# Sums of squares of four heads at once, in float32, on four 32-column groups of TensorE

## The chip, the cores and the metric

The kernel runs on one core of a Trainium2 chip. The metric is the time of one execution on the device, in microseconds (us). Tensors lie in SBUF as partitions by elements; TensorE writes into PSUM. The engines are TensorE (PE, its weight loads PEld), VectorE (DVE), ScalarE (ACT), GpSimd (POOL) and SyncE (SP), which here only issues DMAs.

## The reference, cut to what matters

```python
# x: 16 x 100 x 512, context: 16 x 361 x 256, 16 heads of 128
q = (layernorm(x) @ Wq).reshape(B, Sq, H, D)
k = (ctx @ Wk).reshape(B, Skv, H, D)
v = (ctx @ Wv).reshape(B, Skv, H, D)
q = q * rsqrt(mean(q**2, -1) + eps) * gq       # over the 128 of a head
k = k * rsqrt(mean(k**2, -1) + eps) * gk
attn = softmax(einsum(q, k) / sqrt(D))
x = x + (attn @ v).reshape(B, Sq, H * D) @ Wo
x = x + ffn(layernorm(x))                      # Hadamard, 8-bit activations, ternary weights
```

## The kernel before, in words

There are three stages, one after the other. The first, `queries`, goes over 4 groups of 4 batches (400 tokens) and in each over 16 heads. It makes the queries, stores them to DRAM, and makes the sum of squares of each query. The second, `attention`, goes over 64 units of four heads (16 batches of four units). The third, `feed_forward`, does the output projection and the feed-forward step. The first two are what the change touches.

Nearly all products take float32r operands, each split into a high and a low part: three matmuls (high by high, low by high, high by low) in place of one. psV (`values`), the transposes and a few others have plain float32 operands.

The head's 128 numbers lie on partitions, so the sum of squares is a matmul with a column of ones. Before the change it goes head by head, over four engines:

- ScalarE squares the product out of PSUM into `sq` (L402 in the queries, `square_k` L879 in the attention).
- VectorE casts it to float32r, `sq_hi` (L482, L1015).
- GpSimd subtracts to get the low part, `sq_lo` (L258, L707).
- TensorE runs two float32r matmuls of 128 columns of weights (`squares`, L299 and L766). The weights are a slice of `sel`, which is zero but for one column of ones, at a place that puts the sums of head h on row h of psS (psN in the attention); rows of other heads get zeros added. The heads so add up in one bank, and the last closes it.
- VectorE takes the rows as `ms` (L459, L1025). In the queries TensorE transposes them (psR, L308) to `rq_all`; in the attention SP sends them out and in again so that 76 partitions hold them (`ms_sp`), GpSimd raises them to the power -0.5 (L718), and SP brings the result to all queries as `rk`.

Each engine has its program written out, and the order is set by hand. In the attention a step (one head n) on TensorE is: scores of n (psS), keys of head n + 11 (psK, six matmuls), squares of head n + 9 (psN), transposes of n - 2 (psP), and then either a part of the values of unit u - 2 (psV, steps 0 and 1) or a half of the gather of unit u - 1 (psZ, steps 2 and 3). On ScalarE it is: pr of n - 1, the high part of the keys, the exponential of n, the square, the high part of the transposes. On VectorE: 1/sum of n - 1, ms (step 3), the low part of the transposes, the scaling of the scores with the maximum, the low part of the keys, the negated maximum, the cast. psK has two banks, `sq` two slots.

In the queries a step on TensorE is twelve matmuls for psQ and the squares of the head two before.

Of the kernel before, what the change touches and what calls it, by code (L numbers as in the profile page):

```python
# [22 lines left out]
P = 128  # L23
# [23 lines left out]
TT = P  # L47
TILES = -(-T // TT)
# [3 lines left out]
def build(nc, x, ctxT, ctx_k, wq, wk, wv, wo, gq, gk, w_ff, ident_in, had_in, out):  # L52
# [4 lines left out]
    with ExitStack() as top:  # L57
# [20 lines left out]
        with ExitStack() as ctx:  # L78
# [4 lines left out]
                "sel": sbt(ctx, "sel", [P, 2 * P - 1], F32R),  # L83
# [37 lines left out]
def queries(nc, sbt, sem, passed, weights, ident, rq_all, neg_half, asums, d_q, x, wq, wk, wv, gq, gk, w_ff, ctxT,  # L121
# [7 lines left out]
    with ExitStack() as ctx:  # L129
# [14 lines left out]
        sq = sb("sq1", [P, 2, GT])  # L144
        sq_hi, sq_lo = sb("sq1_hi", [P, 2, GT], F32R), sb("sq1_lo", [P, 2, GT], F32R)
        ms = sb("ms1", [H, GT])
# [3 lines left out]
        psR = ctx.enter_context(nc.psum_tensor("psR", [P, GB, H], F32))  # L150
# [10 lines left out]
        p_q, a_q, v_sqhi, g_sqlo = s("p1_q"), s("a1_q"), s("v1_sqhi"), s("g1_sqlo")  # L161
# [80 lines left out]
        def _(pool):  # L242
            nc.gpsimd.memset(neg_half[:], -0.5).then_inc(g_const, 1)
            nc.gpsimd.memset(sel[:].bitcast(F32), 0.0).then_inc(g_const, 1)
            pool.wait_ge(g_const, 2)
            nc.gpsimd.memset(sel[:, P - 1:P].bitcast(F32), 1.0).then_inc(g_const, 1)
# [9 lines left out]
            def low_squares(g, h):  # L256
                pool.wait_ge(v_sqhi, g * H + h + 1)
# [7 lines left out]
            def group(g, first, last):  # L265
                for h in range(H - 2 if last else H):
                    low_squares(g, h)
# [12 lines left out]
        def _(pe):  # L280
# [66 lines left out]
            squares(G - 1, H - 2)  # L347
            squares(G - 1, H - 1)
# [3 lines left out]
        def _(act):  # L352
# [35 lines left out]
            def group(g, first, last):  # L388
                for h in range(H):
# [10 lines left out]
                    if due(g * H + h - 1):  # L400
                        act.wait_ge(g_sqlo, g * H + h - 1)
                    nc.scalar.activation(sq[:, h % 2, :], psQ[h % 2][:, 0:GT], ACT.Square).then_inc(a_q, 1)  # L402
# [12 lines left out]
        def _(dve):  # L415
# [36 lines left out]
            def factors(g):  # L452
                dve.wait_ge(p_rq, g + 1)
                nc.vector.tensor_copy(rq_all[:, bass.ds(g * GB, GB), :], psR[0:SQ, :, :]).then_inc(v_rq, 1)

            def mean_squares(g):
                dve.wait_ge(p_ss, (g + 1) * H)
                dve.wait_ge(p_rq, g)
                nc.vector.tensor_scalar(ms[:], psS[0:H, 0:GT], D * EPS, None, ALU.add).then_inc(v_ms, 1)  # L459
# [8 lines left out]
            def group(g, first, last):  # L468
                for h in range(H):
# [9 lines left out]
                    dve.wait_ge(a_q, g * H + h + 1)  # L479
                    if due(g * H + h - 1):  # L480
                        dve.wait_ge(p_ss, g * H + h - 1)
                    nc.vector.tensor_copy(sq_hi[:, h % 2, :], sq[:, h % 2, :]).then_inc(v_sqhi, 1)  # L482
                    if last and h >= H - 2:
                        dve.wait_ge(v_sqhi, g * H + h + 1)
# [1263 lines left out]
```

## Time and profile before

| | us |
|---|---|
| median of 3 runs | 1581.12 (1580.83 to 1581.52) |
| profiled execution, its own time | 1577.1 |
| its span | 1575.2 |
| TensorE, busy | 1473.0 (94%) |
| TensorE, weight loads | 1322.9 (84%) |
| VectorE, busy | 1089.8 (69%) |
| ScalarE, busy | 1002.2 (64%) |
| GpSimd, busy | 870.2 (55%) |

A row of a group of instructions gives line, engine, operation, out<-in by the program's names, partitions x elements, the count, the busy time and the mean of one; then the idle time before them and what ended it. Matmuls are pipelined: one is drawn with its whole latency, so they overlap in the rows, and the distance between starts is what one costs. A timeline gives the start, the duration and the number of merged instructions. The profile calls float32r operands of a matmul f32 too. The queries stage ends at about 190 us, the attention at about 1114 us.

### The profile page before, as it was taken

How to read it: one execution, taken by the hardware profiler on the slowest of the kernel's cores; microseconds unless marked ns; L12 is line 12 of the kernel's file. 1: busy time of each engine (PE TensorE's matmuls, PEld its weight loads, DVE VectorE, ACT ScalarE, POOL GpSimd, SP SyncE). 2: the span in 40 equal slices, each digit the busy share in tenths (PEclk: the TensorE clock that was granted, in tenths of full speed). 3: DMA queues.
4: the chain of work that ended last, by engine and by line, in shares of the span. 5: the costliest groups of instructions: out<-in, count | busy, mean ns of one | idle time of the engine just before them, and what ended most of it. 6: DMA issues, size and time to landing. Idle time of an engine off the chain costs nothing. (4 is left out here: it accounts for less than half of the span.)

```text
span 1575.2 us, 31846 instructions
## 1 busy us (share of the span) xinstructions
PE 1473.0 (94%) x9026; PEld 1322.9 (84%) x9026; DVE 1089.8 (69%) x2924; ACT 1002.2 (64%) x2223; POOL 870.2 (55%) x631
## 2 busy tenths in 40 slices
PE   6999979999999999999999999998689999999986
PEld 6999969999999999999999999997566666666753
DVE  6433277778888888788888788775456766566654
ACT  4565568887887778787788787886333344434432
POOL 3477647766666555666566665656135554455523
PEclk9999999999999999999999999999799999999998
DMA  7766512344343344334433344334611112111100
GB/s 233 208 186 196 165 51 76 96 118 112 108 112 100 105 120 116 89 106 119 112 106 107 96 111 120 90 93 121 217 34 34 46 48 67 40 40 53 47 7 14
DMA packets 160333, 158.29 MB, mean 100 GB/s; under 512 B 83585, under 2 KB 134801, under 8 KB 158417
## 3 DMA queue, kind: packets, MB, share of 16 engines
q1 hardware_dynamic: 153296, 144.40, 32.5%
q10 hardware_dynamic: 6912, 12.59, 2.6%
q8 instruction: 36, 0.59, 0.2%
q14 instruction: 89, 0.72, 0.1%
HBM read 123.44 MB, written 33.14 MB: 99 GB/s over the span
## 5 line engine op out<-in xcount | busy, mean ns | idle before, releaser
L707 POOL TENSOR_TENSOR sq_lo<-sq,sq_hi 128x362 fp32r<-128x362 f32 x246 | 284.4, 1156 | 279.0 <-DVE sq_hi L1015 278.7
L718 POOL TENSOR_TENSOR rk_sp<-ms_sp,neg_half 76x10 f32<-76x10 f32 (+1 forms) x128 | 243.6, 1904 | 83.0 <-DMA ms_sp<-ms 82.8
L885 ACT ACTIVATE ex<-sc,nb,rq 100x361 f32<-100x361 f32 x256 | 176.7, 690 | 66.8 <-DVE nb L1057 65.2
L892 ACT ACTIVATE pr<-ex,ri 100x361 f32<-100x361 f32 x256 | 152.8, 597 | 70.6 <-DVE ri L1039 69.9
L755 PE MATMUL psK<-cT_hi,wk_hi 128*128 128x362 f32 x512 | 170.3, 333 | 0.7 <-DVE k_lo L1009 0.7
L755 PE MATMUL psK<-cT_hi,wk_lo 128*128 128x362 f32 x512 | 169.3, 331 | 0.0
L755 PE MATMUL psK<-cT_lo,wk_hi 128*128 128x362 f32 x512 | 169.1, 330 | 0.0
L1029 DVE TENSOR_TENSOR pT_lo<-psP,pT_hi 121x300 fp32r<-121x300 f32 x256 | 117.9, 460 | 66.8 <-ACT pT_hi L900 65.5
L874 ACT ACTIVATE k_hi<-psK 128x362 fp32r<-128x362 f32 x256 | 120.4, 470 | 61.6 <-PE psK L755 57.1
L801 PE MATMUL psZ<-pT_hi,cK_hi 120*128 120x400 f32 (+1 forms) x384 | 143.2, 373 | 0.1
L1050 DVE CUSTOM_DVE_ANT_0 sc<-psS,rk 100x361 f32<-100x361 f32 x256 | 133.6, 522 | 14.0 <-DMA rk<-rk_dram 7.5
L816 PE MATMUL psV<-z,wv_sb 128*128 128x100 f32 x1024 | 136.5, 277 | 1.3 <-issue 0.7
L1009 DVE TENSOR_TENSOR k_lo<-psK,k_hi 128x362 fp32r<-128x362 f32 x256 | 134.8, 526 | 3.1 <-ACT sq L879 2.8
L801 PE MATMUL psZ<-pT_lo,cK_hi 120*128 120x400 f32 (+1 forms) x384 | 132.4, 345 | 0.0
L801 PE MATMUL psZ<-pT_hi,cK_lo 120*128 120x400 f32 (+1 forms) x384 | 131.9, 344 | 0.0
L816 PEld LDWEIGHTS psV<-z,wv_sb 128*128 128x128 f32 x1024 | 125.0, 193 | 2.7 <-issue 2.4
L1258 POOL TENSOR_TENSOR stage<-stage 128x512 f32<-128x512 f32 x26 | 32.5, 1272 | 166.3 <-DVE stage L1656 166.3
L789 PE MATMUL psP<-ident,pr 100*120 100x100 f32 (+1 forms) x768 | 112.8, 255 | 9.4 <-DVE pT_lo L1029 4.4
L879 ACT ACTIVATE sq<-psK 128x362 f32<-128x362 f32 x256 | 116.1, 453 | 0.0
L789 PEld LDWEIGHTS psP<-ident,pr 100*120 100x120 f32 (+1 forms) x768 | 96.4, 159 | 22.3 <-ACT pr L892 13.0
L1656 DVE SCALAR_TENSOR_TENSOR stage<-psB,al,sil 128x512 f32<-128x512 f32 x52 | 38.9, 748 | 109.9 <-ACT sil L1496 109.9
L900 ACT ACTIVATE pT_hi<-psP 121x300 fp32r<-121x300 f32 x256 | 104.6, 409 | 3.0 <-PE psP L789 3.0
(182 smaller groups left out, 4205.7 us busy)
## 6 DMA issues: line engine op xcount, KB each, us to landing
rk<-rk_dram SPq DMA_DIRECT2D x64, 564.1 KB
o_in<-o_dram SPq DMA_DIRECT2D x13, 1024.0 KB, 5.8
q_dram<-q_out SPq DMA_DIRECT2D x64, 200.0 KB, 3.9
q_in<-q_dram SPq DMA_DIRECT2D x64, 200.0 KB, 4.8
o_dram<-o SPq DMA_DIRECT2D x64, 200.0 KB, 5.4
stage<-in_w_ff SPq DMA_DIRECT2D x12, 1024.0 KB, 5.9
w_in<-in_w_ff ACTq DMA_DIRECT2D x48, 256.0 KB, 3.3
cT_in<-in_ctxT SPq DMA_DIRECT2D x16, 361.0 KB, 5.2
```

The source lines that it names most:

```text
L707: nc.gpsimd.tensor_tensor(sq_lo[:, h % 2, :], sq[:, h % 2, :], sq_hi[:, h % 2, :].bitcast(F32), op=ALU.subtract).then_inc(g_sqlo, 1)
L718: nc.gpsimd.tensor_tensor(rk_sp[:, cols], ms_sp[:, cols], neg_half[0:HG * SKR, :].to_broadcast([HG * SKR, n]), op=ALU.pow).then_inc(g_rk, 1)
L755: last = nc.tensor.matmul(psK[h % 2][:, 0:SKP], w[:, c, col:col + D], x[:, slot, c, :], start=(n == 0), stop=(n == 3 * CC - 1))
L789: last = nc.tensor.transpose(psP[0:KW[i], i * SQ:(i + 1) * SQ], pr[:, h % 2, KO[i]:KO[i] + KW[i]], ident[0:SQ, 0:SQ])
L801: last = nc.tensor.matmul(psZ[c][:, 0:UQ], w[0:KW[i], slot, i, c * P:(c + 1) * P], x[0:KW[i], j % 2, i, :], start=(n == 0), stop=(n == 8))
L816: last = nc.tensor.matmul(psV[:, h * SQ:(h + 1) * SQ], wv_sb[:, c, col:col + D], z[:, c, h * SQ:(h + 1) * SQ], start=(c == 0), stop=(c == ...
L874: nc.scalar.activation(k_hi[:, j, h, :], psK[h % 2][:, 0:SKP], ACT.Copy)
L885: nc.scalar.activation(ex[:, h % 2, :], sc[:, h % 2, :], ACT.Exp, bias=nb[:, h % 2:h % 2 + 1], scale=rq[:, j % 2, h:h + 1], accum_out=rs[: ...
L892: nc.scalar.activation(pr[:, h % 2, :], ex[:, h % 2, :], ACT.Copy, scale=ri[:, h % 2:h % 2 + 1]).then_inc(a_pr, 1)
L1009: nc.vector.tensor_tensor(k_lo[:, j, h, :], psK[h % 2][:, 0:SKP], k_hi[:, j, h, :].bitcast(F32), ALU.subtract).then_inc(v_klo, 1)
L1029: nc.vector.tensor_tensor(pT_lo[0:KW[0], j % 2, :, h * SQ:(h + 1) * SQ], psP[0:KW[0], 0:3 * SQ].rearrange("p (i q) -> p i q", q=SQ), pT_hi ...
L1050: nc.vector.tensor_tensor_reduce(out=sc[:, h % 2, :], in0=psS[0:SQ, 0:SK], in1=rk[:, j % 2, h, :], scale=1.0, scalar=-3.0e38, op0=ALU.mult ...
```

## The change

The sums of squares of four heads are made in one block. ScalarE writes the squares of four heads side by side (`sq` has now two slots of four heads), and TensorE, once the fourth is there, runs four float32 matmuls on the plain squares. Each has 32 columns of weights and its own group of 32 columns of the array (`tile_position=(0, 32 * j)`), so the sums of head j of the four land on partitions 32 j and up of the same bank. The cast and the subtraction are gone, with their semaphores. `ms` has now 128 partitions; in the attention the four rows that count are 0, 32, 64 and 96, and SP takes them with a stride; in the queries head 4 k + j lies on partition 32 j + k, psR is a full transpose, and the copy to `rq_all` puts the heads in order. `sel` is 63 float32 columns.

The blocks stand where a head's squares stood, once every four heads: in the queries in steps 1, 5, 9 and 13, in the attention in step 1 of a unit, after the keys. `mean_squares` on VectorE moves from step 3 to step 2. The square on ScalarE waits once per four heads, for the block of the four before last to have read the slot. `feed_forward` is the same in both.

```diff
-                "sel": sbt(ctx, "sel", [P, 2 * P - 1], F32R),
+                "sel": sbt(ctx, "sel", [P, 2 * QW32 - 1]),
...
-            def squares(g, h):
-                pe.wait_ge(g_sqlo, g * H + h + 1)
-                if h == 0:
+            def squares(g, k):
+
+                pe.wait_ge(a_q, g * H + k * HG + HG)
+                if k == 0:
                     if due(g):
                         pe.wait_ge(v_ms, g)
-                for part in (sq_hi, sq_lo):
-                    last = nc.tensor.matmul(psS[:, 0:GT], sel[:, P - 1 - h:2 * P - 1 - h], part[:, h % 2, :],
-                                            start=(h == 0 and part is sq_hi), stop=(h == H - 1 and part is sq_lo))
+                for j in range(HG):
+                    rows = slice(j * QW32, (j + 1) * QW32)
+                    last = nc.tensor.matmul(psS[rows, 0:GT], sel[:, QW32 - 1 - k:2 * QW32 - 1 - k], sq[:, k % 2, j, :],
+                                            start=(k == 0), stop=(k == NG - 1), tile_position=(0, j * QW32))
                 last.then_inc(p_ss, 1)
...
-                    last = nc.tensor.transpose(psR[0:SQ, b, :], ms[:, b * SQ:(b + 1) * SQ], ident[0:H, 0:H])
+                    last = nc.tensor.transpose(psR[0:SQ, b, :], ms[:, b * SQ:(b + 1) * SQ], ident[:])
...
-                    if h >= 2:
-                        squares(g, h - 2)
-                    elif not first:
-                        squares(g - 1, H - 2 + h)
+                    if h % HG == 1 and h > HG:
+                        squares(g, h // HG - 1)
+                    elif h == 1 and not first:
+                        squares(g - 1, NG - 1)
...
-                    nc.vector.tensor_copy(sq_hi[:, h % 2, :], sq[:, h % 2, :]).then_inc(v_sqhi, 1)
...
-                sp.dma_start(ms_sp[:], ms[:].rearrange("h (i k) -> h i k", i=SKR)).then_inc(d_ms, 16)
+                sp.dma_start(ms_sp[:], ms[0:P:QW32, :].rearrange("h (i k) -> h i k", i=SKR)).then_inc(d_ms, 16)
...
-            def low_squares(m, h):
-                pool.wait_ge(v_sqhi, m + 1)
-                nc.gpsimd.tensor_tensor(sq_lo[:, h % 2, :], sq[:, h % 2, :], sq_hi[:, h % 2, :].bitcast(F32),
-                                        op=ALU.subtract).then_inc(g_sqlo, 1)
...
+            def squares(u, j):
+
+                pe.wait_ge(a_k, u * HG + HG)
+                if due(u):
+                    pe.wait_ge(v_ms, u)
+                for h in range(HG):
+                    rows = slice(h * QW32, (h + 1) * QW32)
+                    last = nc.tensor.matmul(psN[rows, 0:SKP], sel[:, QW32 - 1:2 * QW32 - 1], sq[:, j % 2, h, :],
+                                            start=True, stop=True, tile_position=(0, h * QW32))
                 last.then_inc(p_ss, 1)
...
-                    if real(m - 2, HEADS):
-                        hs = (h + LEAD - 2) % HG
-                        squares(m - 2, hs, u + (h + LEAD - 2) // HG)
+                    if (h + LEAD) % HG == 0 and real(u + (h + LEAD) // HG - 1, UNITS):
+                        squares(u + (h + LEAD) // HG - 1, (j + (h + LEAD) // HG - 1) % NG)
...
-            def square_k(m, h):
-                if due(m - 1):
-                    act.wait_ge(g_sqlo, m - 1)
-                nc.scalar.activation(sq[:, h % 2, :], psK[h % 2][:, 0:SKP], ACT.Square).then_inc(a_k, 1)
+            def square_k(m, u, j, h):
+                if h == 0:
+                    if due(u - 1):
+                        act.wait_ge(p_ss, u - 1)
+                nc.scalar.activation(sq[:, j % 2, h, :], psK[h % 2][:, 0:SKP], ACT.Square).then_inc(a_k, 1)
...
-                nc.vector.tensor_scalar(ms[:], psN[0:HG, 0:SK], 1.0 / D, EPS, ALU.mult, ALU.add).then_inc(v_ms, 1)
+                nc.vector.tensor_scalar(ms[:], psN[:, 0:SK], 1.0 / D, EPS, ALU.mult, ALU.add).then_inc(v_ms, 1)
...
-                    if h == 3 and real(u + 2, UNITS):
+                    if h == 2 and real(u + 2, UNITS):
                         mean_squares(u + 2)
...
-                    if real(m - 1, HEADS):
-                        high_squares(m - 1, (h + LEAD - 1) % HG)
```

Where the rows move. First TensorE in the attention, the end of step 1 of a unit. Before:

```order
L755 MATMUL psK<-cT_hi,wk_lo 128x362
L766 MATMUL psN<-sq_hi,sel 128x362
L766 MATMUL psN<-sq_lo,sel 128x362
L789 MATMUL psP<-ident,pr 121x100
L789 MATMUL psP<-ident,pr 120x100 x2
L816 MATMUL psV<-z,wv_sb 128x100 x4
L778 MATMUL psS<-k_hi,q_hi 100x362
```

After, at the same place:

```order
L729 MATMUL psK<-cT_hi,wk_lo 128x362
L741 MATMUL psN<-sq,sel 32x362 x4
L764 MATMUL psP<-ident,pr 121x100
L764 MATMUL psP<-ident,pr 120x100 x2
L791 MATMUL psV<-z,wv_sb 128x100 x4
L753 MATMUL psS<-k_hi,q_hi 100x362
```

The four float32 matmuls of 32 columns of weights stand in place of two float32r ones of 128. In the other three steps the keys are followed by the transposes at once:

```order
L729 MATMUL psK<-cT_lo,wk_hi 128x362
L729 MATMUL psK<-cT_hi,wk_lo 128x362
L764 MATMUL psP<-ident,pr 121x100
L764 MATMUL psP<-ident,pr 120x100 x2
L776 MATMUL psZ<-pT_hi,cK_hi 128x400
```

Second, VectorE in the attention, around ms. `ISA` rows with no name are the counting of passed waits. Before, from the cast of step 2 to the low transposes of step 3 (of a unit that also splits a context):

```order
L1015 CAST sq_hi<-sq 128x362
L989 REGISTER_ALU
L990 TENSOR_TENSOR cT_lo<-cT_in,cT_hi 128x2x361
L1001 REGISTER_ALU
L1002 TENSOR_TENSOR q_lo<-q_in,q_hi 128x400
L1004 ISA
L1004 COPY rq<-rq_all 100x4
L1039 RECIPROCAL ri<-rs 100x1
L1022 ISA
L1024 REGISTER_ALU
L1025 TENSOR_SCALAR ms<-psN 4x361
L1029 TENSOR_TENSOR pT_lo<-psP,pT_hi 121x3x100
```

After, from ms of step 2 to the end of that step:

```order
L991 TENSOR_SCALAR ms<-psN 128x361
L995 TENSOR_TENSOR pT_lo<-psP,pT_hi 121x3x100
L1014 REGISTER_ALU
L1016 ISA sc,mx<-psS,rk 100x361
L1016 ISA mx 100x1
L983 REGISTER_ALU
L984 TENSOR_TENSOR k_lo<-psK,k_hi 128x362
L1023 TENSOR_SCALAR nb<-mx,rq 100x1
L977 TENSOR_TENSOR q_lo<-q_in,q_hi 128x400
L979 ISA
L979 COPY rq<-rq_all 100x4
```

The cast is gone from each step, and ms stands one step earlier in the unit, before the step of q_lo and not after it. GpSimd, which had a `sq_lo` in each step, keeps only the powers of the key factors.

## Rows read from the trace of the kernel before

**Rows 1.** The page, part 1: busy us of each engine, its share, its instructions.
```profile
PE 1473.0 (94%) x9026; PEld 1322.9 (84%) x9026; DVE 1089.8 (69%) x2924; ACT 1002.2 (64%) x2223; POOL 870.2 (55%) x631
```

**Rows 2.** Busy time by stage: queries, steady attention, feed-forward; the first row names the columns.
```profile
core 0: us, PE busy (x) PEld busy (x) DVE busy (x) ACT busy (x) POOL busy (x), PEclk, DMA share, GB/s
20.00:190.00 170.00, 166.64 (x940) 164.30 (x939) 63.04 (x132) 100.47 (x192) 109.81 (x89) 1.00 0.71 207
300.00:1000.00 700.00, 690.54 (x4510) 669.61 (x4508) 578.03 (x1763) 558.15 (x1400) 427.18 (x303) 1.00 0.39 108
1115.00:1575.00 460.00, 404.74 (x2288) 287.91 (x2288) 286.12 (x531) 177.96 (x229) 206.16 (x133) 0.96 0.18 54
```

**Rows 3.** Groups of instructions by form, TensorE, 300 to 1000 us.
```profile
line engine op names shapes xcount | busy us, mean ns | idle before us <-releasers
...
L766 PE MATMUL psN<-sq_hi,sel 128*128 128x362 f32 x201 | 68.9, 343 | 3.3 <-DVE ms L1025 1.8 <-POOL sq_lo L707 0.5
```

**Rows 4.** Timeline, TensorE, a step of the attention: start us, duration us, engine, line, what.
```profile
601.36 0.33 PE L778 MATMUL psS<-k_hi,q_hi 128*100 128x362 f32 x1
...
602.68 0.33 PE L755 MATMUL psK<-cT_hi,wk_lo 128*128 128x362 f32 x1
602.85 0.33 PE L766 MATMUL psN<-sq_hi,sel 128*128 128x362 f32 x1
603.01 0.33 PE L766 MATMUL psN<-sq_lo,sel 128*128 128x362 f32 x1
603.18 0.42 PE L789 MATMUL psP<-ident,pr 100*121 100x100 f32 x3
...
603.36 0.97 PEld L816 LDWEIGHTS psV<-z,wv_sb 128*128 128x128 f32 x8
603.44 1.06 PE L816 MATMUL psV<-z,wv_sb 128*128 128x100 f32 x8
...
605.82 0.33 PE L766 MATMUL psN<-sq_hi,sel 128*128 128x362 f32 x1
```

**Rows 5.** Timeline of the psR block in the queries, TensorE.
```profile
72.80 0.34 PE L299 MATMUL psS<-sq_hi,sel 128*128 128x400 f32 x1
...
72.98 0.35 PE L299 MATMUL psS<-sq_lo,sel 128*128 128x400 f32 x1
...
73.26 0.27 PEld L308 LDWEIGHTS psR<-ident,ms 16*100 16x100 f32 x4 [0.27 <-issue]
73.26 0.36 PE L308 MATMUL psR<-ident,ms 16*100 16x16 f32 x4
...
73.55 0.45 PE L327 MATMUL psQ<-xT_hi,wq_hi 128*128 128x400 f32 x1
...
73.84 0.34 PE L327 MATMUL psQ<-xT_lo,wq_hi 128*128 128x400 f32 x1
```

**Rows 6.** Waits, 300 to 1000 us: engine, line, awaited: us in total, times, longest.
```profile
PEld psP L789 <- ACT pr L892: 6.9, 21, 0.4
...
PEld psN L766 <- POOL sq_lo L707: 6.1, 17, 0.6
PEld psP L789 <- DVE pT_lo L1029: 5.4, 4, 1.6
PEld psN L766 <- DVE ms L1025: 4.3, 9, 0.5
```

**Rows 7.** Timeline, TensorE, float32 transposes of 128 columns in the feed-forward.
```profile
1230.55 0.60 PE L1365 MATMUL psT<-ident,stage 128*128 128x128 f32 x4
```

**Rows 8.** Timeline, ScalarE, the step of rows 4.
```profile
603.77 0.69 ACT L885 ACTIVATE ex<-sc,nb,rq 100x361 f32<-100x361 f32 x1 [0.18 <-DVE nb L1057]
...
604.46 0.45 ACT L879 ACTIVATE sq<-psK 128x362 f32<-128x362 f32 x1
```

**Rows 9.** Groups of instructions, GpSimd and VectorE, 300 to 1000 us.
```profile
L707 POOL TENSOR_TENSOR sq_lo<-sq,sq_hi 128x362 fp32r<-128x362 f32 x200 | 235.2, 1176 | 235.7 <-DVE sq_hi L1015 235.5
...
L1015 DVE CAST sq_hi<-sq 128x362 fp32r<-128x362 f32 x200 | 67.2, 336 | 0.0
```

More of the change, by code:

```diff
@@ L47 @@
 TT = P
+QW32 = P // HG
 TILES = -(-T // TT)
@@ L143, in queries @@
         q_out = sb("q_out", [P, QS, GT])
-        sq = sb("sq1", [P, 2, GT])
-        sq_hi, sq_lo = sb("sq1_hi", [P, 2, GT], F32R), sb("sq1_lo", [P, 2, GT], F32R)
-        ms = sb("ms1", [H, GT])
+        sq = sb("sq1", [P, 2, HG, GT])
+        ms = sb("ms1", [P, GT])
         psQ = [ctx.enter_context(nc.psum_tensor(f"psQ{i}", [P, 512], F32)) for i in range(2)]
@@ L149, in queries @@
         psS = ctx.enter_context(nc.psum_tensor("psS1", [P, 512], F32))
-        psR = ctx.enter_context(nc.psum_tensor("psR", [P, GB, H], F32))
+        psR = ctx.enter_context(nc.psum_tensor("psR", [P, GB, P], F32))
         d_x = [s(f"d1_x{b}") for b in range(GB)]
@@ L265, in group @@
             def group(g, first, last):
-                for h in range(H - 2 if last else H):
-                    low_squares(g, h)
+                for h in range(H):
                     if h == 5 and not last:
@@ L346, in _ @@
             group(G - 1, False, True)
-            squares(G - 1, H - 2)
-            squares(G - 1, H - 1)
+            squares(G - 1, NG - 1)
             factors(G - 1)
@@ L399, in group @@
                     nc.scalar.activation(q_out[:, h % QS, :], psQ[h % 2][:, 0:GT], ACT.Copy, scale=gprod[:])
-                    if due(g * H + h - 1):
-                        act.wait_ge(g_sqlo, g * H + h - 1)
-                    nc.scalar.activation(sq[:, h % 2, :], psQ[h % 2][:, 0:GT], ACT.Square).then_inc(a_q, 1)
+                    if h % HG == 0 and due(g * NG + h // HG - 1):
+                        act.wait_ge(p_ss, g * NG + (h // HG - 1))
+                    nc.scalar.activation(sq[:, h // HG % 2, h % HG, :], psQ[h % 2][:, 0:GT], ACT.Square).then_inc(a_q, 1)
             split_first(0)
@@ L453, in factors @@
                 dve.wait_ge(p_rq, g + 1)
-                nc.vector.tensor_copy(rq_all[:, bass.ds(g * GB, GB), :], psR[0:SQ, :, :]).then_inc(v_rq, 1)
+                nc.vector.tensor_copy(rq_all[:, bass.ds(g * GB, GB), :].rearrange("q b (k j) -> q b k j", k=NG),
+                                      psR[0:SQ, :, :].rearrange("q b (j k) -> q b k j", j=HG)[:, :, 0:NG, :]).then_inc(v_rq, 1)
             def mean_squares(g):
-                dve.wait_ge(p_ss, (g + 1) * H)
+                dve.wait_ge(p_ss, (g + 1) * NG)
                 dve.wait_ge(p_rq, g)
-                nc.vector.tensor_scalar(ms[:], psS[0:H, 0:GT], D * EPS, None, ALU.add).then_inc(v_ms, 1)
+                nc.vector.tensor_scalar(ms[:], psS[:, 0:GT], D * EPS, None, ALU.add).then_inc(v_ms, 1)
             def low_xT(g):
@@ L478, in group @@
                             norm(g + 1, range(2 * (h - 7), 2 * (h - 7) + 2))
-                    dve.wait_ge(a_q, g * H + h + 1)
-                    if due(g * H + h - 1):
-                        dve.wait_ge(p_ss, g * H + h - 1)
-                    nc.vector.tensor_copy(sq_hi[:, h % 2, :], sq[:, h % 2, :]).then_inc(v_sqhi, 1)
-                    if last and h >= H - 2:
-                        dve.wait_ge(v_sqhi, g * H + h + 1)
-                        dve.wait_ge(g_sqlo, g * H + H - 2)
-                        nc.vector.tensor_tensor(sq_lo[:, h % 2, :], sq[:, h % 2, :], sq_hi[:, h % 2, :].bitcast(F32),
-                                                ALU.subtract).then_inc(g_sqlo, 1)
                     if h == 1 and not first:
@@ L601, in pipeline @@
                 unit(UNITS + j, B, j, 0)
-        def early(m):
-            return isinstance(m, int) and m < LEAD - 1
         def first_batch(b):
@@ L731, in unit @@
                 for h in range(HG):
-                    m = u * HG + h + LEAD
-                    if real(m - 1, HEADS) and not early(m - 1):
-                        low_squares(m - 1, (h + LEAD - 1) % HG)
                     if h == 0 and real(u + 1, UNITS):
@@ L758, in keys @@
                 last.then_inc(p_k, 1)
-            def squares(m, h, v_ms_count):
-                pe.wait_ge(g_sqlo, m + 1)
-                if h == 0:
-                    if due(v_ms_count):
-                        pe.wait_ge(v_ms, v_ms_count)
-                for part in (sq_hi, sq_lo):
-                    last = nc.tensor.matmul(psN[:, 0:SKP], sel[:, P - 1 - h:2 * P - 1 - h], part[:, h % 2, :],
-                                            start=(h == 0 and part is sq_hi), stop=(h == HG - 1 and part is sq_lo))
+            def squares(u, j):
[6 more added lines that the diff above has]
+                                            start=True, stop=True, tile_position=(0, h * QW32))
                 last.then_inc(p_ss, 1)
```

29 lines of the change are left out of this document (8 added, 21 removed).

## The prediction

> **What bounds the kernel now.** I read the share of busy time first [rows 1], then the same by stage [rows 2]. TensorE is busy 94% of the span, and its weight loads 84%. By stage: the queries (20 to 190 us) have it 166.64 of 170 us busy, the steady attention (300 to 1000 us) 690.54 of 700, the feed-forward step (from 1115 us) 404.74 of 460. VectorE, ScalarE and GpSimd stand at 83%, 80% and 61% in the attention. So in the two stages that the diff touches a microsecond of TensorE is close to a microsecond of the kernel. The feed-forward step isn't touched; I let it stand.
>
> Busy time hides short waits, though: a 362-column matmul is drawn 0.33 us long, but the next starts 0.165 us later [rows 4]. So I count starts, not durations. A unit is four heads, and 201 heads lie in these 700 us [rows 3]: 13.9 us each. The waits [rows 6] show what is hidden: before psN, TensorE's loads waited 6.1 us for sq_lo and 4.3 for ms, and before psP 6.9 + 5.4. About 50 units lie there, so the first two come to 10.4 / 50 = 0.21 us a unit.
>
> **The change, part by part.** *Removed on TensorE.* Eight float32r matmuls of 362 columns per unit: psK at 602.68, psN at 602.85 and 603.01, psP at 603.18, so 0.166 us each [rows 4], 1.33 us a unit. In the queries eight of 400 columns, 0.18 us each (72.80, 72.98 [rows 5]): 1.44 us per four heads.
>
> *Added on TensorE.* Four float32 matmuls on 32-column groups, one block per four heads. No float32 matmul of that width and no column group is in the trace; three unknowns, each bounded from rows.
>
> First, the float32 stream. psV has four matmuls by the order and x8 records in the trace [rows 4]: a float32 matmul runs as two records. These follow each other at (1.06 - 0.275) / 7 = 0.112 us for 100 columns, beside weight loads of 128 columns. The transposes, one record each, take (0.42 - 0.25) / 2 = 0.086 us for 100 columns [rows 4], and (0.60 - 0.276) / 3 = 0.108 for 128 [rows 7]: 0.85 ns a column, against 0.166 / 362 = 0.46 for float32r. A record of 362 columns is then 0.31 us (0.41 at psV's rate, and 0.166 if it ran like float32r). I take 0.31, since psV's 0.112 equals its own weight loads (0.97 us for eight) and here the loads are 32 columns. For 400 columns it is 0.345 us.
>
> Second, how much of the four groups runs side by side. Full overlap is two records, 0.62 us; none is eight, 2.48 us; the case between is a rival below. I take full overlap: in a block no group needs what another has, each writes its own 32 partitions of psN, and all four squares are there before it starts.
>
> Third, the change of array shape on the way in and out. The nearest row is the psR block, whose operands have 16 rows [rows 5]: the last psS started at 72.98 and streams to 73.16, but the weight load of psR starts only at 73.26; the psQ behind it is in step again at 73.66 (the second starts at 73.84, less 0.18). The block took 0.49 us for four matmuls 0.05 us apart, so 0.29 us went into the two changes. It could be 0 if columns behave otherwise, or 0.5 if the first records also lose their preloaded weights. I take 0.29. The Trainium skill (TensorEngine Tiling, Key Properties) says that changing the tiling mode drains the engine. The psR row agrees that something of that size is lost; no row shows it for columns.
>
> Per unit, then: 0.62 + 0.29 - 1.33 = -0.42 us, times 64 units = -27 us. In the queries: 0.69 + 0.29 - 1.44 = -0.46, times 16 blocks = -7 us. psR becomes a full 128-row transpose of 100 columns per batch: four times (0.086 - 0.05) dearer per group, and without its own 0.29; over four groups -1 us at most, taken as 0 with the wider copy behind it.
>
> *Waits.* The psN waits on sq_lo and ms go: 64 x 0.21 = 13 us if nothing takes their place. The psP waits on pr and pT_lo remain and come sooner when TensorE is faster; I give 5 of the 13 back: -8 us. The new wait is for the square of the head just before. In this step ScalarE ended it at 604.46 + 0.45 = 604.91, and TensorE comes to psN at 605.82 [rows 4, 8]: 0.9 us to spare, still 0.57 with the two psN matmuls gone from the step before. Behind it on TensorE stand psP and psV or psZ of the step, and ScalarE waits for psP. I cost it at nothing; if the cover fails by 0.5 us in each unit it is +32 us, which is part of the second rival.
>
> *Removed elsewhere.* VectorE's cast, 200 x 336 ns in 700 us, 1.3 us a unit, and GpSimd's subtraction, 1176 ns a head [rows 9]. Neither engine is the bound, so their time is worth nothing itself. VectorE goes from 83% of 13.9 us to 10.2 of 13.2, 77%; GpSimd keeps only the powers. In the queries VectorE mostly waits already. ScalarE's square now waits once a unit for the block of the unit before, a long time past. ms is computed on 128 partitions, 361 elements each as before, in a step one head earlier on VectorE: there it can wait for the block just issued, and behind it stand pT_lo and the scaling of scores. TensorE reaches the end of the block about 1.5 + 0.9 us after the first scores matmul of its step (601.36 to psN at 602.85, and the block); VectorE gets there after the exponential of that step, which ends 3.1 us after the scores (603.77 + 0.69) [rows 4, 8]. I cost it at nothing, and at 0.1 us a unit if a step runs early, 6 us. SP's DMA of ms moves the same four rows, now from partitions 32 apart; two units of lead cover it.
>
> *The ends.* The last two heads of the queries no longer go square, cast, subtraction, matmul: about 1 us off, once.
>
> Sum: -27 - 7 - 8 - 1 = **-43 us**. The profiled execution took 1577.1 us, which gives 1534; the median of the runs is 1581.1, 4 us above it, which gives **1538 us**. The ends of what this case leaves unknown: with nothing for the shape and all waits recovered -45 - 12 - 13 - 1 = -71, 1510 us; with 0.5 us for the shape and none recovered -13 - 4 - 1 = -18, 1563 us. Records at 0.41 us would add 2 x 0.1 x 80 blocks = 16 us, and at 0.166 take 23 off; both stay inside 1510 to 1563 with the middle shape.
>
> **Rivals.** *A: the two records of one group hold up the next group.* If records start in order and the second of a group must wait for the first on the same columns, only the second of one group overlaps the first of the next: five records in a row. 5 x 0.31 + 0.29 - 1.33 = +0.51 a unit, +33; queries 5 x 0.345 + 0.29 - 1.44 = +0.57, +9; the sq_lo and ms waits fully gone, since all others have more slack, -13: +29, **1610 us**. It decides as soon as the block is over 1.33 us plus the waits recovered, 1.5 us. For it: two records per matmul in [rows 4] with a weight load each; against it: nothing in the trace. The Trainium skill (TensorE: Matmul & The Clock Gate, Part 3) says matmuls start and end strictly in program order, and also that tiles in different column groups start about 4 ns apart, with 2.38x measured for three. The first would lead here, the second to my forecast; those tests had, as described, one matmul per tile.
>
> *B: the overlap is there, but half the gain is eaten.* TensorE then waits for pr and pT_lo. These chains already hold it 12.3 us in 700 [rows 6], and ScalarE's work per unit (80% of 13.9 = 11.1 us) doesn't shrink. Or the new wait for the square costs 0.3 us a unit (+19). -43 + 22: **1560 us**.
>
> *C: column groups don't overlap at all.* 8 x 0.31 + 0.29 - 1.33 = +1.44 a unit, +92; queries +1.61, +26; waits -13: +105, **1686 us**.
>
> *D: nothing moves*, since two waits of 0.2 us trade places with the shorter block: within 3 us of 1581.
>
> **How the numbers follow.** Forecast 0.50, A 0.25, B 0.13, C 0.07, D 0.05. The likeliest's own range is 1510 to 1563; the range that holds eight in ten has to take in A and leaves out C and the outer part of the low end: 1516 to 1612. A 0.2% difference, 3 us, is about what timing tells from none. Faster: forecast and B, less a little, 0.61; same: D with the edges of A and B, 0.07; slower: A and C, 0.32.
>
> **What would show it.** In the profile after: eight psN records a unit, each about 0.31 us of stream. In the forecast their starts fall in at most two clusters and the psP behind starts some 0.9 us after the block's first; in A the block is 1.7 to 1.9 us, in C 2.8. The units should lie 13.3 us apart against 13.9. The load of psP should start late by about 0.1 us, as psR's does. The waits should list psN <- ms and sq_lo no more; if psN <- ACT sq stands there with more than 10 us, the cover has failed. The feed-forward stage should keep its 460 us. I'm wrong if a psN record takes over 0.41 us, if the block exceeds 1.3 us, or if ScalarE sets the pace.

## The result, and the profile after

| | before | after |
|---|---|---|
| median, us | 1581.32 (1580.83 to 1585.69, 4 runs) | 1524.95 (1522.29 to 1527.65, 4 runs) |
| profiled execution, its own time / its span | 1577.1 / 1575.2 | 1525.7 / 1523.9 |

The ratio is 0.9638, with a 95% interval of 0.9613 to 0.9662: 56 us faster by the medians, 51 by the profiled executions. Beside the experiments the kernel before took 1579.5 to 1580.2 us; the kernel after was measured beside the result alone, so differences to it below, which go by medians, are good to some 2 us.

The page of the kernel after, part 1, answers to [rows 1]:

```profile
PE 1424.7 (93%) x9026; PEld 1220.8 (80%) x9026; DVE 942.1 (62%) x2592; ACT 988.5 (65%) x2223; POOL 523.1 (34%) x323
```

TensorE's records are as many as before, 9026: eight float32r matmuls became four float32 ones of two records each. By stage, as in [rows 2], with the last stage 53 us earlier:

```profile
20.00:190.00 170.00, 162.63 (x951) 143.92 (x949) 36.35 (x68) 99.62 (x193) 42.15 (x27) 1.00 0.74 208
300.00:1000.00 700.00, 694.18 (x4765) 645.41 (x4764) 509.23 (x1643) 579.76 (x1480) 203.06 (x107) 1.00 0.41 112
1062.00:1523.00 461.00, 406.99 (x2288) 287.89 (x2286) 285.12 (x528) 176.97 (x227) 206.04 (x132) 0.96 0.19 54
```

In the attention GpSimd fell from 427 to 203 us of 700 and VectorE from 578 to 509, while TensorE stayed full. The first scaled product of the last stage (psA, wk_hi by o_hi; line, operation, count, ns, first and last start) shows how much was won up to there; before, then after:

```profile
L1305 PE MATMUL psA<-wk_hi,o_hi x104: 387/389/767, 1115.5 to 1499.3; 128*128 128x512 f32 x104
```

```profile
L1269 PE MATMUL psA<-wk_hi,o_hi x104: 387/389/764, 1061.4 to 1445.2; 128*128 128x512 f32 x104
```

The last stage starts 54.1 us earlier. The first keys (psK) start at 191.8 us before and 190.2 after, so 1.6 us of it come from what lies ahead of the attention (the queries stage is 3.1 us shorter, but its first matmul starts 1.4 us later) and 52.5 from the attention; the feed-forward step gives 3 back, though nothing in it changed (its length differs by as much between other kernels here).

*The block.* Timeline of TensorE after, a step with a block, to be laid beside [rows 4]; the eight records of psN are merged:

```profile
607.17 0.32 PE L729 MATMUL psK<-cT_hi,wk_lo 128*128 128x362 f32 x1
607.42 0.82 PE L741 MATMUL psN<-sq,sel 128*32 128x362 f32 x8
608.16 0.52 PE L764 MATMUL psP<-ident,pr 100*121 100x100 f32 x3
608.52 0.50 PE L791 MATMUL psV<-z,wv_sb 128*128 128x100 f32 x3
```

psN would be due at 607.17 + 0.166 = 607.34 and starts 0.08 later; psP starts at 608.16, and the next group 0.36 behind it in place of 0.26 [rows 4], so psP lost another 0.10. The block costs 608.16 + 0.10 - 607.34 = 0.92 us; the forecast had 0.91. The eight records start in two clusters, the second 0.33 us behind the first; by tile (ns min/median/max, first and last start) and, from the timeline, the second four:

```profile
L741 PE MATMUL psN<-sq,sel x8: 467/480/493, 607.4 to 607.8; 128*32 128x362 f32 x8
```

```profile
607.75 0.49 PE L741 MATMUL psN<-sq,sel 128*32 128x362 f32 x4
```

In the queries:

```profile
63.69 0.34 PE L323 MATMUL psQ<-xT_hi,wq_lo 128*128 128x400 f32 x1
63.96 0.88 PE L295 MATMUL psS<-sq,sel 128*32 128x400 f32 x8
64.77 0.45 PE L323 MATMUL psQ<-xT_hi,wq_hi 128*128 128x400 f32 x1
65.05 0.34 PE L323 MATMUL psQ<-xT_lo,wq_hi 128*128 128x400 f32 x1
```

From 63.69 + 0.18 to 65.05 - 0.18: 1.00 us, forecast 0.98.

*The units.* Starts of the first scores matmul of a unit, before (the next unit's is the first of [rows 4], 601.36), then after, three units in a row:

```profile
587.90 0.33 PE L778 MATMUL psS<-k_hi,q_hi 128*100 128x362 f32 x1
```

```profile
577.08 0.33 PE L753 MATMUL psS<-k_hi,q_hi 128*100 128x362 f32 x1
...
590.13 0.33 PE L753 MATMUL psS<-k_hi,q_hi 128*100 128x362 f32 x1
...
603.19 0.33 PE L753 MATMUL psS<-k_hi,q_hi 128*100 128x362 f32 x1
```

After, these units take 13.05 and 13.06 us, and all take 13.03 to 13.14 but the first two, the last two and the four at a jump back of the loop (15.2 to 15.4). Before, this one took 601.36 - 587.90 = 13.46, near the shortest; by the starts of psS in the same trace the regular units run from 13.42 to 14.12 us in a turn of four, 13.78 on average between the first jump back and the end of the loop, against 13.06 after. (The mean by [rows 3], 700 / 50.25 = 13.93, has the units at the jumps in it.) So 0.40 us of a unit is the shorter block, and 0.32 is waits. The waits after (300 to 1000 us, all of TensorE's but psV's; beside [rows 6]):

```profile
PEld psP L764 <- issue: 28.2, 48, 0.6
...
PEld psN L741 <- issue: 12.0, 53, 0.2
...
PEld psP L764 <- DVE pT_lo L995: 5.9, 4, 1.5
PE psP L764 <- DVE pT_lo L995: 5.1, 6, 1.2
PEld psP L764 <- ACT pr L867: 4.6, 9, 0.6
```

The two rows "issue" are the change of array shape, already in the 0.92. psN waits for nobody: neither for `ms` nor for ScalarE's square. What is left for pT_lo and pr falls almost wholly on the four places where the attention's loop jumps back. For pT_lo that is no less than before (5.9 us on the weight loads against 5.4); the waits that went are those of psN and, for pr, 6.9 us down to 4.6. These lists miss a part of each wait: a matmul is drawn about 0.16 us longer than the distance to the next, and a delay within that leaves no idle time.

*VectorE beside GpSimd.* Two groups of VectorE, before and then after, 300 to 1000 us (as in [rows 9]):

```profile
L985 DVE SCALAR_TENSOR_TENSOR w_out<-w_in,bound,below 128x512 fp8e4<-128x512 f32 x48 | 59.4, 1238 | 7.3 <-DVE below L982 6.3
L1004 DVE COPY rq<-rq_all 100x4 f32 (+1 forms) x50 | 47.4, 949 | 0.0
```

```profile
L960 DVE SCALAR_TENSOR_TENSOR w_out<-w_in,bound,below 128x512 fp8e4<-128x512 f32 x48 | 36.1, 752 | 7.3 <-DVE below L957 6.3
...
L979 DVE COPY rq<-rq_all 100x4 f32 (+1 forms) x53 | 8.7, 164 | 0.0
```

Neither was edited. A copy of 100 x 4 elements took 0.95 us and takes 0.16 now. The timeline before tells why:

```profile
610.21 0.91 DVE L990 TENSOR_TENSOR cT_lo<-cT_in,cT_hi 128x722 fp32r<-128x722 f32 x1
610.38 2.06 POOL L707 TENSOR_TENSOR sq_lo<-sq,sq_hi 128x362 fp32r<-128x362 f32 x1 [2.33 <-DVE sq_hi L1015]
...
611.03 0.57 DVE L1002 TENSOR_TENSOR q_lo<-q_in,q_hi 128x400 fp32r<-128x400 f32 x1
...
611.52 0.95 DVE L1004 COPY rq<-rq_all 100x4 f32 x1
...
612.45 0.50 DVE L1025 TENSOR_SCALAR ms<-psN 4x361 f32<-4x361 f32 x1
...
613.01 0.43 PE L766 MATMUL psN<-sq_hi,sel 128*128 128x362 f32 x1 [0.18 <-DVE ms L1025]
```

The copy starts inside GpSimd's subtraction and ends with it (612.47 against 612.44). `ms` behind it starts late, and TensorE waits for `ms`. It works the other way too: this subtraction takes 2.06 us where most take 0.97 to 1.16, and it ends 0.84 us behind the end of q_lo (611.60). All twelve subtractions that start under cT_lo and q_lo take 2.06 us in these 700 us.

That the two engines hold each other up is what the Trainium skill states (SBUF — State Buffer, "SBUF: two separate sides"): they share one port pair, which is locked for a whole instruction, and the other fully blocks; on VectorE's side this holds for instructions in a two-port mode, or with two inputs in SBUF while GpSimd reads SBUF. The row agrees in that the end of the copy is the end of the subtraction. w_out, with two inputs in SBUF, agrees less closely: at 600.48 it started under a subtraction that ran until 601.17, and it ended at 601.72, 0.55 us later, where it takes 0.75 alone.

What this did to the chain that feeds TensorE stands in ScalarE's waits, 300 to 1000 us, before and then after. ScalarE makes pr from VectorE's 1/sum (ri), and TensorE's psP needs pr:

```profile
ACT pr L892 <- DVE ri L1039: 64.0, 98, 3.1
```

```profile
ACT pr L867 <- DVE ri L1005: 3.2, 1, 3.2
```

Of the 98 waits 48 (43 us) stand in the step in which ri is right behind w_out and 50 (21 us) in the one in which it is right behind rq; in the other two steps of a unit there is none.

### The profile page after: what moved, and what is told of

Read it like the earlier page. It is cut to its first block and busy times, and to the rows that moved or that the text cites. A ratio compares the mean times of both kernels' runs of the same rounds, so it can differ in the third digit from the quotient of the medians.

```text
span 1523.9 us, 30817 instructions
## 1 busy us (share of the span) xinstructions
PE 1424.7 (93%) x9026; PEld 1220.8 (80%) x9026; DVE 942.1 (62%) x2592; ACT 988.5 (65%) x2223; POOL 523.1 (34%) x323
## 5 line engine op out<-in xcount | busy, mean ns | idle before, releaser
L1005 DVE RECIPROCAL ri<-rs 100x1 f32<-100x1 f32 x256 | 41.4, 162 | 143.5 <-ACT ex L860 133.9
L729 PEld LDWEIGHTS psK<-cT_hi,wk_hi 128*128 128x128 f32 x512 | 97.0, 189 | 4.2 <-DVE k_lo L984 3.3
```

Source lines behind the costliest of these rows:

```text
L729: last = nc.tensor.matmul(psK[h % 2][:, 0:SKP], w[:, c, col:col + D], x[:, slot, c, :], start=(n == 0), stop=(n == 3 * CC - 1))
```

## The experiments

All edits are against the kernel after unless the text says otherwise; ratios are to the kernel before.

### One stage at a time

> The change in the queries alone, the attention as before. The profile after shows 170 us from the first query matmul to the last before and 169 after, so the stage gave far less than the 7 us of my sum. Theory 1 (TensorE there now waits for the square of the last head, so most of the gain is lost): 2 to 4 us faster than before, 1577 to 1579. Theory 2 (the 7 us are there, and the profiled execution hid them): 1574.

Edit: `queries` of after with `attention` of before. Measured 1583.97 us, ratio 1.0032 (1.0018 to 1.0045): 4 us slower by the medians, which neither theory had.

> The change in the attention alone, the queries as before. By the distance of units in the two profiles (13.9 and 13.2 us) it holds nearly all: 64 x 0.75 = 48 us off, 2 more at the start of the stage, and 3 given back in the feed-forward if that is real: 1528 to 1532. If the gain of the queries were the 7 us of my sum it would have to be 1533 or more for the whole change to end at 1525.

Edit: `queries` of before with `attention` of after. Measured 1529.08, ratio 0.9681 (0.9664 to 0.9699), as expected.

The attention alone brings 50 of the 56 us, and the queries on top of it some 4 more. The queries alone bring nothing: their stage is 3 us shorter (first psQ to first psK 173.6 us against 177.0), but the attention behind it, untouched, is 9 us longer in that trace (first psK to first psA 933 us against 924), which I can't explain. In the queries 16 blocks x 0.44 = 7 us of TensorE's work went and 3 to 4 were seen. A part of the rest stands in the waits of after, 20 to 190 us:

```profile
PEld psQ L323 <- issue: 13.2, 19, 1.7
...
PEld psQ L323 <- ACT sq L397: 4.3, 7, 1.2
...
PE psQ L323 <- ACT sq L397: 3.2, 4, 1.4
```

In the queries a step without squares is now 2.2 us of TensorE, and ScalarE has two instructions of a head and often half a sum of weights in it. Before, TensorE's psQ is in none of the waits; only psS waited there, its weight loads 2.2 us for GpSimd's sq_lo and 1.7 for VectorE's.

### Column groups or the full array

> The changed kernel with the same four float32 matmuls in the same place, but each over all 128 columns of the array (one column of ones at row 32 h), so no column groups and no change of shape. If float32 costs two records of 0.31 us and they follow each other: block 8 x 0.31 = 2.48 us against 0.93, +1.55 x 64 = +99, and in the queries (2.76 - 0.98) x 16 = +28: 1525 + 127 = 1652, less up to 10 for waits that vanish behind the longer block. If float32 records of this width ran at the rate of float32r (0.166 us), the block would be 1.33 us and the time some 1550.

```diff
-    rows = slice(h * QW32, (h + 1) * QW32)
-    last = nc.tensor.matmul(psN[rows, 0:SKP], sel[:, QW32 - 1:2 * QW32 - 1], sq[:, j % 2, h, :],
-                            start=True, stop=True, tile_position=(0, h * QW32))
+    row = h * QW32
+    last = nc.tensor.matmul(psN[:, 0:SKP], sel[:, P - 1 - row:2 * P - 1 - row], sq[:, j % 2, h, :],
+                            start=(h == 0), stop=(h == HG - 1))
```

(the same in the queries). Measured 1647.64, ratio 1.0431 (1.0412 to 1.045), as expected. The block, timeline of TensorE:

```profile
614.58 0.33 PE L729 MATMUL psK<-cT_hi,wk_lo 128*128 128x362 f32 x1
614.74 2.60 PE L741 MATMUL psN<-sq,sel 128*128 128x362 f32 x8
617.18 0.42 PE L764 MATMUL psP<-ident,pr 100*121 100x100 f32 x3
```

(617.18 - 614.74) / 8 = 0.305 us a record, and no change of shape ahead or behind. With the same operands the groups save 2.44 - 0.92 = 1.52 us a block; the regular units are 1.51 us longer (14.58 against 13.07). In all it is 123 us by the medians, of which some 14 lie in the four units at a jump back, beyond the block's part: they take 4.0 to 6.6 us more than the others here. Float32 alone, without groups, would have been 4% slower than before.

### Half as many records

> The column-group kernel with the squares written by ScalarE in float16 and a float16 selector: four matmuls of one record each per block in place of four of two records (the squares are rounded to float16, so the sums carry that error). The block went 0.31 (first four records) + 0.31 (second four) + 0.3 for the change of shape. If the two groups of records are the cost, as the trace shows, the block goes to 0.15 + 0.3 us: -0.46 us a unit, x64 = -30 in the attention, -5 in the queries: 1490. Rival: the waits psP <- pr and pT_lo eat half, since ScalarE's work a unit does not shrink: 1505 to 1510. Second rival: ScalarE's Square costs more when it writes float16, over 1515.

```diff
-                "sel": sbt(ctx, "sel", [P, 2 * QW32 - 1]),
+                "sel": sbt(ctx, "sel", [P, 2 * QW32 - 1], FP16),
-        sq = sb("sq2", [P, 2, HG, SKP])
+        sq = sb("sq2", [P, 2, HG, SKP], FP16)
```

(and `sq1` likewise). Measured 1508.31, ratio 0.9552 (0.9529 to 0.9575). Timeline of TensorE, then two of its waits, 300 to 1000 us:

```profile
607.88 0.32 PE L730 MATMUL psK<-cT_hi,wk_lo 128*128 128x362 f32 x1
608.13 0.34 PE L742 MATMUL psN<-sq,sel 128*32 128x362 f16 x4
608.40 0.52 PE L765 MATMUL psP<-ident,pr 100*121 100x100 f32 x3
608.75 0.28 PE L792 MATMUL psV<-z,wv_sb 128*128 128x100 f32 x1
```

```profile
PEld psP L765 <- ACT pr L868: 13.7, 43, 0.8
...
PE psP L765 <- DVE pT_lo L996: 8.8, 15, 1.5
```

The block is 608.40 + 0.09 - 608.05 = 0.44 us: 0.48 less, as forecast from the records. The kernel kept 17 of the 35 us. The queries kept 4 of 5; in the attention three units of four are mostly 0.3 to 0.4 us shorter, and every fourth only 0.0 to 0.2. psP now waits 13.7 us for pr in place of 4.6. That is the rival that was named, within its 1505 to 1510.

### Where the waits went

The cast and the subtraction are put back, in memory that is free at that time; TensorE waits for neither. ScalarE's square waits for the subtractions of a unit earlier, and VectorE's cast for the subtraction of two heads before.

> The changed kernel, but in the attention VectorE and GpSimd still do the cast and the subtraction of each head (up to head 236 of 256), into spare memory, and TensorE waits for neither. Theory 1 (the waits of TensorE went because it no longer depends on the two): within 3 us of the changed kernel, 1523 to 1528. Theory 2 (the 17 us that the attention gained above the block's own 27 come from VectorE's 1.3 us a unit being free): most of them is lost again, 1537 to 1543.

```diff
+            def high_squares(m, j, h):                       # VectorE, after negate_max
+                nc.vector.tensor_copy(sq_hi[:, h % 2, :], sq[:, j % 2, h, :]).then_inc(v_sqhi, 1)
+            def low_squares(m, j, h):                        # GpSimd, at the start of a step
+                pool.wait_ge(v_sqhi, m + 1)
+                nc.gpsimd.tensor_tensor(sq_lo[:, h % 2, :], sq[:, j % 2, h, :], sq_hi[:, h % 2, :].bitcast(F32),
+                                        op=ALU.subtract).then_inc(g_sqlo, 1)
```

Measured 1592.04, ratio 1.0071 (1.0043 to 1.0098). Both theories missed, by 49 us and more: TensorE and ScalarE show no wait for this work, VectorE one of 0.5 us in 700, and it costs 67 us. One way is through GpSimd: the powers of the key factors stand in its queue among the subtractions, and VectorE's scaling of scores waits 19.0 us for rk in these 700, where it has no such wait in the kernel after.

> The column-group kernel with VectorE's cast and GpSimd's subtraction kept (TensorE waits for neither), and ms in step 3 of a unit as in the kernel before, in place of step 2. With ms in step 2 it took 1592 us. Theory O: ms one step early stands in the way of the other heavy instructions of step 2 on VectorE, and the powers on GpSimd hold up the subtractions behind them: 1570 to 1582 here, since TensorE has 0.4 us a unit less to do than in the kernel before. Theory W: the two engines' load together is the cause, wherever ms stands: 1588 to 1596.

```diff
-                    if h == 2 and real(u + 2, UNITS):
+                    if h == 3 and real(u + 2, UNITS):
                         mean_squares(u + 2)
```

Measured 1572.32, ratio 0.9966 (0.9939 to 0.9993); its profiled execution was slower than that, 1579.9. Theory O held: with the loads in place the early `ms` costs 20 us, and the wait for rk falls from 19.0 to 5.0. Its regular units take 13.70 us over the same stretch in which those of the kernel before take 13.78: with the loads there, the block that is 0.40 us shorter gains next to nothing. TensorE's waits in it, 300 to 1000 us:

```profile
PEld psP L775 <- ACT pr L879: 49.7, 101, 1.0
...
PE psP L775 <- DVE pT_lo L1012: 17.2, 19, 3.1
PEld psP L775 <- DVE pT_lo L1012: 10.4, 4, 3.4
```

psP waits 50 us for pr, pr waits 65.6 us for VectorE's 1/sum, nearly what it waited before (64.0), and w_out is 1.22 us again.

> The column-group kernel, to which VectorE's cast of each head's squares is added back in the attention (heads 1 to 235, into memory that is free there); TensorE waits for none of it, and GpSimd keeps only the powers. With the cast and GpSimd's subtraction both added the kernel took 1592 us against 1525. Theory V: it was VectorE's own time (0.34 us a head, 1.3 us a unit): then this kernel alone gives most of it back, 1565 to 1590. Theory G: it was GpSimd, whose long subtractions hold back the powers behind them and stretch VectorE's instructions (w_out 1.24 us against 0.75, rq 0.95 against 0.16, together 1.25 us a unit): then the cast alone costs little, 1525 to 1535. Theory M: VectorE has some 2.5 us a unit to spare and either load alone fits: 1525 to 1540 here and in the next kernel.

Edit: only `high_squares`. Measured 1527.92, ratio 0.9673 (0.9657 to 0.9688). Units of 13.06 us, as without it. Both G and M held, and V fell.

> The column-group kernel, to which one GpSimd subtraction per head of the old size (128x362, into free memory, its two inputs the square itself) is added back in the attention, without VectorE's cast; TensorE waits for none of it. Theory G: 1575 to 1595, VectorE's w_out and rq back at 1.24 and 0.95 us. Theory V: 1525 to 1535. Theory M: 1525 to 1540, with w_out and rq long again.

Edit: only `low_squares`, which waits for ScalarE's square and subtracts it from itself. Measured 1556.35, ratio 0.983 (0.9791 to 0.9869), outside the range of every theory.

```profile
L973 DVE SCALAR_TENSOR_TENSOR w_out<-w_in,bound,below x36: 750/752/754, 406.1 to 892.7; 128x512 fp8e4<-128x512 f32 x36
```

(line, operation, count, ns min/median/max, 400 to 900 us.) Theory G was right that it is GpSimd's load that costs, and wrong on the way: w_out is not stretched at all, and rq in only 6 of 51 copies (0.75 to 1.50 us in place of 0.16). Without the cast ahead of it the subtraction starts at ScalarE's square and is done when w_out comes; it also takes 0.79 us here against 1.16, so this is less than the old load. Theory V falls: VectorE's 1.3 us a unit alone are free. Theory M is half right: most units take 13.06 us here too. Of the 28 us between the first and the last unit, some 10 lie in the four units at a jump back (15.9 to 19.2 us), 5.6 in the two units ahead of three of them, 6 in one stretch of six units from 446 to 531 us, and 5.5 in the first two and the last; in the other units the subtraction is free. So what this kernel tells is that the subtraction makes disturbances longer, not that it slows each unit.

Together: cast +3 us, subtraction +31, both +67 (+47 with `ms` later). The sum of the single ones is 34. With both, the subtraction starts just when VectorE's cast ends, so it lies over what VectorE does next, w_out and rq, and there the regular units are longer too (13.80 us, 13.70 with `ms` later, against 13.06). What makes the disturbances longer I can't name in full: the trace of the subtraction alone shows the scaling of scores waiting 4.9 us for rk, since the powers stand in GpSimd's queue behind the subtractions, and waits for pT_lo of up to 3.8 us, mostly where the loop jumps back. No run has the loads kept and the loop written out, so how much of the 67 and 31 us belongs to the jumps was not tested.

### Two more edits, and the jumps back

> The column-group kernel with the absolute sums of the feed-forward weights in the queries taken by VectorE in place of ScalarE. In the queries the change gained 2 to 3 us where 7 were forecast. Theory 1: the rest is lost since TensorE's next scores wait for ScalarE's last square of the four, with the sums ahead of it: then 3 to 5 us come off, 1520 to 1522. Theory 2: the queries are held by the loads of x and the transposes, or the sum on VectorE takes the place of the wait: 1525 or more.

Edit: `sum_ff` of the queries on VectorE (tensor_reduce with absolute values) in place of ScalarE. Measured 1540.59, ratio 0.9734 (0.9711 to 0.9757): within theory 2's number, but not for its reason. The wait for ScalarE's square went from 7.5 to 2.1 us and the queries gained 2 us (first psQ to first psK 172.1 against 173.9); the attention, not edited, is 24 us longer (first psK to first psA 895 against 871). Its other units are 13.06 us as in the kernel after; by the starts of psS the four units at a jump back take 6.7 to 8.1 us more than those, where they took 2.1 to 2.4 more. Timeline of VectorE there, behind w_out, after and then this kernel:

```profile
631.56 0.16 DVE L1005 RECIPROCAL ri<-rs 100x1 f32<-100x1 f32 x1 [2.40 <-issue]
```

```profile
634.50 0.16 DVE L1005 RECIPROCAL ri<-rs 100x1 f32<-100x1 f32 x1 [2.54 <-issue]
...
638.99 0.53 DVE L1016 CUSTOM_DVE_ANT_0 sc<-psS,rk 100x361 f32<-100x361 f32 x1 [3.49 <-issue]
```

VectorE stands 2.4 us at the jump with no wait that the profile shows, and in this kernel 3.5 us more at the fourth instruction behind it.

> The column-group kernel with eight VectorE memsets of 128x1 ahead of the attention, 0.5 us in all, which move VectorE's loop body by as many places in its instruction stream. With the sums of absolute weights on VectorE the attention, in which nothing was changed, took 20 us more, all of it at the four jumps back (7 to 8 us each against 2.2). Theory L: what a jump back costs hangs on where VectorE's stream stands: the jumps here cost another amount than 2.2 us, 3 to 8, and the time is 1529 to 1548. Theory N: the position doesn't matter, it was something that the sums left behind: 1525 to 1527.

```diff
+            for i in range(8):
+                nc.vector.memset(pad[:, i:i + 1], 0.0)
```

Measured 1526.05, ratio 0.9653 (0.9628 to 0.9677). The jumps cost 2.2 to 3.4 us here: nearly theory N. Eight instructions more do not bring a stall of that size; what in the sums on VectorE does stays open. Nor is that kernel alone in it: the units at a jump back are 4.0 to 6.6 us longer in the full-array kernel, in which nothing of VectorE was edited, so an explanation by VectorE's stream alone would not do.

> The column-group kernel with the attention's loop over pairs of batches written out, so that no engine jumps back. In the column-group kernel a unit takes 13.1 us, and the four units at a jump back 2.1 to 2.4 us more, in which VectorE stands idle 2.4 us with nothing to wait for. Theory J: the jump back itself costs this: 4 x 2.2 = 9 us off, 1516. Theory F: the instructions have to be brought in either way, and a stream without a loop stalls elsewhere: 1525 or more.

```diff
-            with eng.Fori(2, B // 2 - 1) as pair:
+            for pair in range(2, B // 2 - 1):
```

Measured 1515.88, ratio 0.9595 (0.9574 to 0.9617): theory J. The 9 us are by the medians (7 by the two ratios), and 8.6 by the four units, which take 13.05 to 13.11 us here. VectorE at that place in this kernel:

```profile
626.13 0.75 DVE L960 SCALAR_TENSOR_TENSOR w_out<-w_in,bound,below 128x512 fp8e4<-128x512 f32 x1
626.80 0.15 DVE L1005 RECIPROCAL ri<-rs 100x1 f32<-100x1 f32 x1
```

> Squares and selector in float16 (the sums carry that rounding) and the attention's loop written out. If both add up: 1508 - 10 = 1498 us. If the stalls at the jumps only move elsewhere: 1508.

Both edits together. Measured 1492.26, ratio 0.944 (0.9418 to 0.9462), the fastest kernel of the study: 33 us under the kernel after, and 6 under what was expected if both add up. Its sums of squares carry float16's rounding of the squares, which the others do not.

## Why the prediction was right, and where its sizes were off

The forecast was 1538 us (own range 1510 to 1563); measured 1524.95. For the block the mechanism was the forecast's; for the waits, nearly half of the gain, it was not. Term by term:

- **The block, -27 us.** Right. 0.92 us against 0.91; (1.33 - 0.92) x 64 = 26 us, and 0.40 us of a unit by the starts.
- **Full overlap.** Right. Rival C is priced by the full-array kernel: 2.44 us a block. Rival A would have been five records in a row, 1.5 us and the change of shape, where eight take 0.92 with it. That a float32 matmul is two records did not hinder it. Rival D is out by the result.
- **Change of shape, 0.29 from the psR block.** Holds for columns too: 0.92 - 2 x 0.305 = 0.31, and with one record each, if it runs in the 0.166 us of [rows 4], 0.44 - 0.17 = 0.27.
- **The queries, -7.** Mis-sized, 3 to 4 by the length of the stage. The block is 0.44 us shorter as said, but psQ now waits for ScalarE (7.5 us), which the prediction had not looked for there. The queries' edit alone gained nothing in the time of the whole (1584 us).
- **The waits, -8.** This is the term that was mis-sized. Attention 52.5 us less 26 for the block leaves some 26: about 21 in waits within the units (0.32 or 0.33 us each) and 5 at both ends of the stage. Two steps of the prediction failed. The first is the price of the waits: the prediction says that it counts starts, but takes them from the list of idle times, 0.21 us a unit. By starts the regular units before lay 0.36 us above the shortest of them (13.78 against 13.42), and after 0.03. The second is the sentence "Neither engine is the bound, so their time is worth nothing itself". The 13 us that TensorE spent waiting for sq_lo and ms were only the end of it. The chain 1/sum, pr, psP runs through VectorE, whose w_out and rq stood 0.5 and 0.8 us longer in each unit under GpSimd's subtraction: (1238 - 752) x 48 + (949 - 164) x 50 = 63 us in 700, and ScalarE's pr waited 64 us for it in just these steps. The gain there needs the loads gone: with them kept and `ms` where it was, the kernel takes 1572, so the shorter blocks and queries alone bring 8 us (5 by the ratio, with an interval of 1 to 10), and dropping the loads, with `ms` a step early, 47. The terms don't add; as these runs read, whichever of TensorE and that chain is slower sets the unit, and the change shortened both. I gave 5 of 13 us back to pr and pT_lo; in truth pr fell too, from 6.9 to 4.6 us, and pT_lo stayed at 5.4 and 5.9, at the jumps alone.
- **New wait for the square, 0; `ms` a step early, 0.** Both right for the kernel as it is: no such row. The second is right for the kernel without the loads: with them kept, the same move costs 20 us.
- **Rival B, half the gain eaten,** is what happened one step further on, with float16: 17 of 35 us came.

The sum was -43 and the result -56 by the medians, -51 by the profiled executions. The waits brought some 18 us more than their 8, the queries 3 to 4 less than their 7, and the feed-forward step took 3 back: that the total came as near as it did is partly that these errors have opposite signs.

## What to carry to other kernels

An engine at 80% that nobody seems to wait for can still set the pace: when a step is taken off VectorE or GpSimd, look for other VectorE instructions that lie inside GpSimd's, and for copies of a few elements that take a microsecond. Count them as part of the chain that they stand in. Count waits too by the distance of starts, from the shortest unit to the mean one. And a shorter piece on the fullest engine pays only as far as the next chain is short too; keep each load in place once, to see which of two gains was the real one.

## What the runs showed that I had not expected

- Eight records on four column groups cost 0.31 us (first four) + 0.31 (second four) and 0.3 us for going in and out of the shape. The price of the shape was the same with four records in the block (0.27 us) as with eight, so it wants few, large blocks: it is a third of the float32 block and two thirds of the float16 one.
- At a jump back of the loop VectorE stands 2.4 us with no wait that the profile shows in the kernel after, and 2.0 in the one before (the row below); writing out the loop's five rounds gained 9 us. The units at these jumps were 2.1 to 2.4 us longer than the others in the kernel after, 4.0 to 6.6 in the full-array kernel, and 6.7 to 8.1 in the kernel in which only an earlier stage was edited. A kernel's loop edges have to be compared before a difference of 20 us is given to the edit. VectorE before, at such a place:

```profile
659.04 0.16 DVE L1039 RECIPROCAL ri<-rs 100x1 f32<-100x1 f32 x1 [1.99 <-issue]
```

- GpSimd's subtraction took 0.97 us at its shortest kind, 1.16 under w_out, 2.06 under cT_lo and q_lo, and 0.79 with one tensor as both inputs and no cast ahead.
